# A scratch tensor kept in the scan's own channel order, and one weight loaded a stage later

## The reference, cut to what matters

```
xn     = layernorm(x)
x1     = xn @ w1_w.T + w1_b
x_conv = silu(depthwise_conv(x1, conv_w))          # 3 taps along the tokens
x_ssm  = ssm(x_conv, A, B, C, D)                   # per channel, 16 states:
         #   h = h * sigmoid(A) + x_t * B ;  y_t = sum_s(h * C) + D * x_t
v      = silu(xn @ v1_w.T + v1_b)
x      = x + (x_ssm * v) @ w2_w.T + w2_b  + quantised_linear(xn, weight, bias)
```

## Time and profile before

| | |
|---|---|
| runs, median | 2282.05 us (2277.57 to 2284.62) |
| profiled execution | 2283.17 us, of which the span of the profile is 2281.4 us |
| busy: PE, PEld, DVE, ACT, POOL | 91%, 70%, 63%, 48%, 33% |
| granted PE clock, mean | 0.948 |
| DMA, mean | 122 GB/s |

### The profile page before, as it was taken

The page is one execution under the profiler, slowest core; times in us unless marked ns, Lnnn a source line. Parts: engine busy times, 40 slices in busy tenths (PEclk is TensorE's granted clock), DMA queues, the critical chain, the costliest instruction groups (busy, mean ns, idle before and its releaser), DMA issues.

```text
span 2281.4 us, 27703 instructions
## 1 busy us (share of the span) xinstructions
PE 2065.9 (91%) x9243; PEld 1594.3 (70%) x9243; DVE 1431.8 (63%) x2869; ACT 1093.1 (48%) x1843; POOL 759.4 (33%) x778
## 2 busy tenths in 40 slices
PE   9999997545445699999999999999999999999998
PEld 6888884111111478888888888888888888888887
DVE  6998863322322366666666666657777667776676
ACT  4555554101211255555555555575545555455543
POOL 1011111111111234444434444414454444544445
PEclk9999999667776799999999999999999999999999
DMA  5666745333233344444435444352212222122210
GB/s 200 242 222 209 222 152 171 104 111 124 92 97 100 100 140 130 139 130 139 130 109 164 126 140 126 110 185 93 66 65 79 88 93 65 65 84 92 85 37 38
DMA packets 214591, 277.38 MB, mean 122 GB/s; under 512 B 46897, under 2 KB 145457, under 8 KB 211889
## 3 DMA queue, kind: packets, MB, share of 16 engines
q1 hardware_dynamic: 202080, 251.83, 33.8%
q10 hardware_dynamic: 12368, 23.79, 2.9%
HBM read 169.53 MB, written 101.83 MB: 119 GB/s over the span
## 4 chain that ended last, share of the span: by engine, by line
PE 76%; ACTq 13%; ACT 3%; DMA 3%; DVE 2%; issue 1%; POOL 1%; SPq 0%; POOLq 0%; DVEq 0%
PE bank L105 21%; PE bank L107 21%; PE bank L106 21%; ACTq L869 9%; PE bank L1591 7%; ACTq L892 3%; PE bank L2135 3%; ACT c_y L865 2%; PE bank L1553 1%; DMA scr_y<-c_y 1%; ACTq L90 1%; PE bank L923 1%; PE bank L944 0%; DMA bv_row<-in_L_attn_bv 0%; ACTq L882 0%
## 5 line engine op out<-in xcount | busy, mean ns | idle before, releaser
L923 PE MATMUL bank<-c_z,c_toep 64*64 64x512 f32 x256 | 58.9, 1008 | 176.4 <-ACT c_y L865 176.4
L105 PE MATMUL bank<-e_ring,e_w_hi 128*128 128x512 f32 x512 | 200.7, 392 | 0.0
L106 PE MATMUL bank<-e_ring,e_w_hi 128*128 128x512 f32 x512 | 199.3, 389 | 0.0
L107 PE MATMUL bank<-e_ring,e_w_lo 128*128 128x512 f32 x512 | 199.2, 389 | 0.0
L796 DVE TENSOR_TENSOR_SCAN c_state<-decay,bank 128x255 f32<-128x255 f32 x128 | 79.6, 668 | 182.8 <-PE bank L944 177.7
L1591 PE MATMUL bank<-d_kh,d_nat 128*128 128x512 f32 x768 | 192.0, 399 | 1.1 <-issue 1.1
L865 ACT ACTIVATE c_y<-bank 128x512 f32<-128x512 f32 x64 | 38.0, 594 | 276.1 <-issue 160.5
L1855 POOL TENSOR_TENSOR e_x<-e_x,e_beta 128x512 f32<-128x512 f32 x64 | 91.5, 1451 | 217.5 <-ACT e_y L1898 217.5
L1591 PEld LDWEIGHTS bank<-d_kh,d_nat 128*128 128x128 f32 x768 | 139.7, 188 | 29.0 <-issue 1.3
L1909 ACT ACTIVATE e_kr<-bank 128x512 f32<-128x512 f32 x64 | 38.0, 593 | 243.8 <-PE bank L107 243.8
L923 PEld LDWEIGHTS bank<-c_z,c_toep 64*64 64x64 f32 x256 | 9.4, 187 | 206.2 <-ACT c_y L865 205.0
(11 more groups left out here) (215 smaller groups left out, 6255.8 us busy)
## 6 DMA issues: line engine op xcount, KB each, us to landing
scr_v<-b_vt SPq DMA_DIRECT2D x64, 256.0 KB, 2.7
scr_z<-b_zt SPq DMA_DIRECT2D x64, 256.0 KB, 2.1
c_z<-scr_z SPq DMA_DIRECT2D x64, 256.0 KB, 5.7
scr_y<-c_y ACTq DMA_DIRECT2D x64, 256.0 KB
d_x<-in_L_attn_x SPq DMA_DIRECT2D x64, 256.0 KB, 5.3
d_v<-scr_v SPq DMA_DIRECT2D x32, 512.0 KB, 5.7
scr_x<-d_x SPq DMA_DIRECT2D x64, 256.0 KB, 3.2
scr_xnt<-d_xt SPq DMA_DIRECT2D x32, 512.0 KB, 4.2
```

The lines of the kernel that those rows point to most:

```text
L105: eng.matmul(out, lhs[hi], rhs[hi], start=first, stop=False, skip_group_check=onto)
L106: eng.matmul(out, lhs[hi], rhs[lo], start=False, stop=False, skip_group_check=onto)
L107: return eng.matmul(out, lhs[lo], rhs[hi], start=False, stop=last, skip_group_check=onto)
L923: yield pe.matmul(bank[i][k * HALF:(k + 1) * HALF, :], tables[o % TABS][rows, :, :].rearrange("p e s -> p (e s)"), zo[o % Z][rows, :], sta ...
```

## The change

The tensor y stays in memory in the order in which the scan produces it: channel position (p, i, k, e) in place of (p, k, i, e). The store of a tile then writes one contiguous block of 128 rows, where it wrote 2 blocks of 64. The host permutes the columns of v1_w, the entries of v1_b and the rows of w2 by the same list `paired`, so v is produced in that order too. The four pieces of Wv leave the scan; ACT issues them in the mixing stage at token tiles 10 to 13, and PE waits for them in `values(b)` only.

```
-    y_of = scr["y"].rearrange("(p k i e) m n -> p i k (e m) n", k=2, i=2, e=EIGHTHS)
+    y_of = scr["y"].rearrange("(o c) m n -> o (c m) n", c=OCTET)
...
         def store(o):
             act.wait_ge(y_done, o + 1)
-            act.dma_start(y_of[o // 2, o % 2], yo[o % Y][:, :]).then_inc(y_stored[o % Y], 16)
+            act.dma_start(y_of[o], yo[o % Y][:, :]).then_inc(y_stored[o % Y], 16)
...
-        pieces = [(w2_raw, "L0_attn_w2_w", raw_in[0]), (wk_raw, "L1_attn_Wk", raw_in[1]),
-                  (wv, "L1_attn_Wv", late["wv_in"])]
+        pieces = [(w2_raw, "L0_attn_w2_w", raw_in[0]), (wk_raw, "L1_attn_Wk", raw_in[1])]
...
-            if WEIGHT_PIECES_AT <= o < WEIGHT_PIECES_AT + 2 * 3 * KT and (o - WEIGHT_PIECES_AT) % 2 == 0:
+            if WEIGHT_PIECES_AT <= o < WEIGHT_PIECES_AT + 2 * 2 * KT and (o - WEIGHT_PIECES_AT) % 2 == 0:
...
-    WEIGHT_HIGH_AT, WEIGHT_LOW_AT = 50, 51
+    WEIGHT_HIGH_AT, WEIGHT_LOW_AT, VALUES_AT = 50, 51, 10
...
             set_keys(N - 2)
+            if N - VALUES_AT in range(KT):
+                kt = N - VALUES_AT
+                act.dma_start(wv[:, kt, :], ins["L1_attn_Wv"][:, kt, :]).then_inc(late["wv_in"], 16)
...
         def values(b):
+            pe.wait_ge(late["wv_in"], 16 * KT)
...
-        pe.wait_ge(late["wv_in"], 16 * KT)
...
+    paired = np.arange(512).reshape(OCT // 2, 2, 2, OCTET // 2).transpose(0, 2, 1, 3).reshape(-1)
...
+        if name == "L0_attn_v1_w":
+            turned = turned[:, paired]
+        if name == "L0_attn_w2_w":
+            turned = turned[paired]
```

More of the change, by code:

```diff
@@ L2318, in by_state @@
         return a.reshape(OCT // 2, 2, 2, OCTET // 2, -1).transpose(1, 3, 4, 0, 2).reshape(-1, OCT)
+    paired = np.arange(512).reshape(OCT // 2, 2, 2, OCTET // 2).transpose(0, 2, 1, 3).reshape(-1)
     laid = {name: a for name, a in raw.items() if name not in PACKED}
     for name in TURNED:
-        laid[name] = raw[name].T.reshape(KT, P, 512).transpose(1, 0, 2)
-    laid["cols"] = np.concatenate([per_partition(raw[n]) for n in COLUMNS]
+        turned = raw[name].T
+        if name == "L0_attn_v1_w":
+            turned = turned[:, paired]
+        if name == "L0_attn_w2_w":
+            turned = turned[paired]
+        laid[name] = turned.reshape(KT, P, 512).transpose(1, 0, 2)
+    laid["cols"] = np.concatenate([per_partition(raw[n][paired] if n == "L0_attn_v1_b" else raw[n]) for n in COLUMNS]
                                   + [per_partition(raw["L0_attn_conv_w"])], axis=1)
```

## The result

| | before | after |
|---|---|---|
| runs, median | 2281.82 us (2277.57 to 2284.62, 4 runs) | 2048.95 us (2046.73 to 2050.40, 4 runs) |
| ratio | | 0.898, 95% interval 0.8963 to 0.8997 |
| profiled execution, span | 2283.17, 2281.4 us | 2047.82, 2046.0 us |
| busy PE, DVE, ACT | 91%, 63%, 48% | 98%, 70%, 53% |
| mean PE clock | 0.948 | 0.997 |

The forecast was 2061 us. The span fell by 235.4 us. Four stretches of the traces add up to it: the scan from its second `within` to the first product of the mixing stage, 362.6 us before, 151.5 after (211.1); the step from that product to the first one on the last 128 channels, 29.8 before and 9.9 after (19.9); 2.1 us earlier at the scan's second `within`; and 2.4 us elsewhere.

A forecast was written before the change was run, and what follows sets the result against it. It took y's stores, on two DMA engines, to bound the scan. Scan terms summed to 160.6 us against 362.6, a gain of 202.0; with 20.1 at its end, 222.1 off 2283.2 gave 2061 us, 8-in-10 range 2036 to 2112.

The forecast's parts named there:

- What bounded the kernel: Scan: y's stores use two of 16 DMA engines, so each issue waits 4.32 us for room in ACT's queue.
- The store after: Scan: y's store spreads over 16 engines, 0.7 us of transfer; issue 0.5 us, landing 3.2 us, queue never full.
- PE's round: Scan: PE sets the round at 4.16 us; 30 rounds and a last `within` and `out_of` of 3.0 make 127.8 us.
- ACT between the takes: Scan, even octets: issues of pieces and biases, splits, bank fills and normalisations add 11.5 us.
- PE's extras: Scan: 16 transposes, 3.5 us, and two bank openings, 1.8 us, add 5.3 us.
- z's loads: Scan: rounds waiting for loads of z to land add 6 us, between ends of 0 and 15.
- rival 1: Scan: z's loads and y's stores collide and rounds follow the loads, 39 us more, 2100 us; chance 0.15.
- DVE: Scan: a wait for a turning transfer, 5 us, and quantising steps and low parts, 5 us, add 10 us.
- The end of the scan: Step into the mixing stage: 42 products hide the last store, 29.8 us becomes 9.7, a gain of 20.1 us.
- Wv's pieces: Mixing stage: four issues of 0.5 us fit ACT's idle time and cost 0; 15 us if the queue were full.
- rival 3: Scan: stores stay on two engines, only Wv's pieces leave, four times 1.9 us and more, 2275 us; chance 0.04.
- Rival 2: Scan: PE's clock does not stay up, 2158 us over the whole scan, 2110 for half the time; chance 0.13.

The follow-up runs named there:

- layout_alone: Against the kernel before, only the new order of y with permuted weights; Wv's four pieces stay in the scan: 2053.37 us, ratio 0.9003.
- two_halves: Changed kernel with y's old memory order and unpermuted weights, each store issued as two transfers of 64 rows: 2054.49 us, ratio 0.9011 to the kernel before.
- z8: Changed kernel with eight tiles for z instead of six, so each load is issued a round earlier: 2029.39 us, ratio 0.8893 to the kernel before.
- z8_late: Changed kernel with eight tiles for z and load_front issued at octet 63 instead of 60: 2025.65 us, ratio 0.8879 to the kernel before.
- wv_alone: Kernel before with only Wv's pieces moved to the mixing stage, y's stores as before: 2279.35 us, ratio 0.9991.

## Why the prediction was right, and where it was off

- **What bounded the kernel.** Right: two engines for the stores, and ACT's queue held by them. layout_alone, two_halves and the row of 2, 4, 8 and 128 rows as the outermost dimension show it.
- **The store after.** Right in kind: the queue is never full. The issue is 0.33 us, not 0.5. Its landing is 5.2 us, not 3.2, which cost nothing behind four tiles of `yo`.
- **PE's round.** I took 4.16 us, the sum of the row lengths. Rows overlap, and the distance between starts is 3.84 us: 30 x 0.32 = 9.6 us too much. The starts of the rows before, 383.15, 384.17 and 386.08, had it: 1.02 + 1.91 and then one more piece below 1.09. The last `within` and `out_of` are 2.4 us, not 3.0.
- **ACT between the takes.** I took 11.5 us (the items as listed make 11.7). A piece's issue runs while ACT copies the bank, both from 401.79, so it is not added. In z8, where z is out of the way, the first 15 rounds take (440.09 - 379.41) / 15 = 4.05 us, 3.1 over 15 times 3.84, and the transposes are in these 3.1. Eleven pieces stood there in my count, 5.5 us.
- **PE's extras.** I took 5.3 us. They are 3.5; the means of the earlier trace rows, 361 and 1022 ns, were taken in part at the lower clock, and are 279 and 598 now:

```profile
L957 PE MATMUL bank<-consts,c_wf_nat 128*128 128x128 f32 x16 | 2.5, 279 | 0.0
...
L1560 PE MATMUL bank<-d_w 128*128 128x512 f32 x2 | 1.0, 598 | 0.0
```

- **z's loads.** I took 6 us and gave 15 as the far end; z8 took 19.6 out, z8_late 23.3. This is the term that was mis-sized, and rival 1 was a part of the truth. The landing was no worse than I assumed, 5.0 us in the median. What was: the spread (2.7 to 9.3 us), which a mean can't show, since a round waits for the later of two loads, the microsecond from the landing to PE's start, and `load_front` between z's last loads, which I had not seen as a cost at all. How the 23 us divide over these no run tells, but for the 11.1 of `load_front` alone.
- **DVE.** I took 10. The remainder in z8's scan is 131.4 - 30 x 3.84 - 2.4 = 13.8 us. 3.5 of it is the one round that still waits for z. The other 10.3 are for PE's extras, ACT, and DVE with POOL together, 26.8 in my count, and are not separated further. PE's waits for DVE and POOL in z8's scan are small (total, times, longest):

```profile
PE bank L945 <- DVE c_state L798: 2.1, 5, 0.8
PE bank L945 <- POOL c_toep L777: 1.3, 2, 0.6
```

- **The end of the scan.** 29.8 - 9.9 = 19.9, forecast 20.1.
- **Wv's pieces.** The step that failed is the count of 1.9 us a piece in the old scan: wv_alone shows 0.57, the rest of that round was z's. The forecast's sum did not rest on it, only rival 3's price did. In the mixing stage they cost nothing, as forecast: an issue is 0.34 us, the landing is 3.1 us, and PE is busy 50.00 of the 50 us in which they are loaded.
- **The clock.** Right: 1.0 nearly throughout. In the scan it was low only at the start and behind the gap at 513 us, where the `own` of 519.90 takes 1.98 us in place of 1.09. Rival 2 did not come about, though PE had idle times of 0.15 to 1.84 us ahead of `own` in 17 of 31 rounds. The Trainium skill, "TensorE: Matmul & The Clock Gate", section "A second HAM failure mode: psum-queue depth-cycling", tells of a kernel whose short idles between groups of products let the clock swing. This trace shows such idles and no swing, 1.00 in each 10 us from 380 to 510 us.
- **Sum.** In the scan the errors are +9.6 for PE's round, +0.6 for its end, +16.5 for PE's extras, ACT and DVE together, and -17.6 for z (20.1 us between the scans of z8 and of the changed kernel, and the 3.5 left, against 6). They make 9.1 us, 160.6 forecast against 151.5. The 4.5 us outside the scan and its end I had not forecast. The forecast was right by its mechanism, and its closeness is in part luck: terms of 17 us each cancelled.

## What to carry to other kernels

Where a queue's issue of a transfer takes microseconds, read how many DMA engines it uses: share times 16, per queue, in a stretch where little else moves. Then look at the outermost dimension on both sides of the transfer. Splitting a store in two, or letting a scratch tensor keep the order in which it is produced and permuting the weights on the host, is cheap. Engines loaded by one bad pattern also delay every other transfer, so count packets on the fullest engine, of all queues. And after a stall has gone, look at how early the loads are issued before you blame the bandwidth: here eight tiles in place of six, with the same bytes, took 19.6 us out.

## What the runs showed of the hardware that was not expected

- A 256 KB store issued by ACT takes 0.33 us to issue as one block of 128 rows, 0.53 as 4 blocks and 0.59 as 8 blocks (medians); a store of 64 rows takes 0.57.
- The DMA moved 319 GB/s of loads and stores at once over 60 us, with PE busy 59.41 of them.
- Transfers of another queue lengthen the issue of a store on two engines by their packets on these engines: 4.32 us alone, 5.62 beside z's two loads (16 packets on each engine), 6.89 beside four such loads (32).
- A queue with room hides a slow pattern from its issuer: with four engines the issues are short and the wait moves to the landing, 108.6 us in 42 waits.
